# The first LayerNorm of an attention layer: where its statistics, power, scaling and maxima stand in the issue order

## What is computed

```
x = layernorm(x + local_attention(x))   # 16 heads of 64, q and k normed, rotary, windows of 128
x = layernorm(x + int8_linear(x))       # its input scale is max(abs(x)) over all of x
x = layernorm(x + linear_attention(x))
x = layernorm(x + bitlinear_ffn(x))
```

## Time and profile before

| | |
|---|---|
| median of three runs | 3080.65 us |
| profiled execution: its own time, its span | 3083.32 us, 3081.5 us |
| PE, DVE, ACT, POOL busy | 2928.3, 2364.4, 2176.6, 1663.0 us |
| PE busy as a share of the span | 95% |
| chain that ended last: PE, ACT, DVE | 21%, 8%, 4% of the span |
| TensorE clock granted | 0.988 of full speed over the span |

### The profile page before, as it was taken

One profiled execution on the slowest core, in us unless ns is written; L12 is line 12 of the kernel. 1 busy time (PEld: TensorE's weight loads), 2 busy tenths in 40 slices (PEclk: granted clock), 3 DMA queues, 4 the chain that ended last, 5 costly groups with the idle time before them and its releaser, 6 DMA issues. The chain is left out here.

```text
span 3081.5 us, 60397 instructions
## 1 busy us (share of the span) xinstructions
PE 2928.3 (95%) x20143; PEld 2313.1 (75%) x20143; DVE 2364.4 (77%) x6845; ACT 2176.6 (71%) x5670; POOL 1663.0 (54%) x2226
## 2 busy tenths in 40 slices
PE   7999999999999999999999996899999999999996
PEld 5777777777777777777777774578888888888885
DVE  7887877877877877877877874787777777777775
ACT  5676766766766766766766763577888888888884
POOL 5655655655655655655655654344555555555555
PEclk9999999999999999999999998899999999999999
DMA  2000000000000000000000002000000000000000
GB/s 84 8 15 22 9 15 20 10 15 15 15 15 15 15 15 15 15 15 15 15 15 15 8 25 86 21 15 8 15 15 15 21 22 15 15 14 15 8 15 21
DMA packets 51219, 57.51 MB, mean 19 GB/s; under 512 B 3008, under 2 KB 48592, under 8 KB 50912
## 3 DMA queue, kind: packets, MB, share of 16 engines
q1 hardware_dynamic: 47904, 50.67, 5.1%
q10 hardware_dynamic: 3008, 2.98, 0.3%
HBM read 36.86 MB, written 16.78 MB: 17 GB/s over the span
## 5 line engine op out<-in xcount | busy, mean ns | idle before, releaser
L642 POOL TENSOR_SCALAR a_ex<-a_ex,a_rc 128x384 f32<-128x384 f32 (+1 forms) x1024 | 538.5, 538 | 551.3 <-DVE a_rc L542 551.3
L434 ACT ACTIVATE a_ex<-a_sm,a_nm 128x384 f32<-128x384 f32 (+1 forms) x1024 | 573.0, 562 | 57.9 <-DVE a_nm L535 40.2
L535 DVE CUSTOM_DVE_ANT_0 a_sm<-sc,a_mask,a_rn 128x384 f32<-128x384 f32 (+1 forms) x1024 | 530.2, 544 | 8.9 <-PE sc L303 8.9
L626 POOL TENSOR_TENSOR a_qr<-a_ra,a_rb 128x256 f32<-128x256 f32 x512 | 370.4, 734 | 227.5 <-DVE a_rb L515 227.4
L440 ACT ACTIVATE a_pt<-tp 128x256 f32<-128x256 f32 (+1 forms) x512 | 221.5, 433 | 283.8 <-PE tp L322 283.7
L267 PE MATMUL pj<-a_whi,a_xhi 128*128 128x384 f32 x1024 | 391.1, 382 | 8.4 <-DVE a_wlo L187 5.1
L1718 POOL TENSOR_TENSOR b_alo<-b_ring,b_ahi 128x512 fp32r<-128x512 f32 x128 | 169.5, 1325 | 414.0 <-DVE b_ring L1547 388.2
L267 PE MATMUL pj<-a_whi,a_xlo 128*128 128x384 f32 x1024 | 346.6, 338 | 0.0
L267 PE MATMUL pj<-a_wlo,a_xhi 128*128 128x384 f32 x1024 | 345.7, 338 | 0.0
L303 PE MATMUL sc<-a_kT,a_qT 64*64 64x256 f32 (+1 forms) x4096 | 307.9, 416 | 1.6 <-DVE a_nm L535 0.9
L332 PE MATMUL qk<-a_pt,a_v 128*64 128x384 f32 (+1 forms) x2048 | 305.6, 441 | 0.6 <-DVE a_pt L547 0.6
(11 more groups left out here) (234 smaller groups left out, 8007.2 us busy)
## 6 DMA issues: line engine op xcount, KB each, us to landing
a_xres<-x SPq DMA_DIRECT2D x16, 512.0 KB, 3.8
y<-a_res SPq DMA_DIRECT2D x16, 512.0 KB, 2.9
b_y<-y SPq DMA_DIRECT2D x16, 512.0 KB, 3.9
a_xin<-x SPq DMA_DIRECT2D x15, 512.0 KB, 3.8
out<-b_y SPq DMA_DIRECT2D x15, 512.0 KB, 2.9
a_xin<-wqkv SPq DMA_DIRECT2D x8, 256.0 KB, 2.6
a_stage<-wqkv SPq DMA_DIRECT2D x3, 384.0 KB, 9.1
a_ot<-wqkv ACTq DMA_DIRECT2D x3, 384.0 KB, 12.0
```

The lines of the kernel that those rows point to most:

```text
L434: e.activation(ex[h][w][:, 0:width], sm[h][w % 2][:, 0:width], ACT.Exp, bias=nm[:, w, h:h + 1], scale=-1.0, accum_out=rs[:, w, h:h + 1]).t ...
L535: e.tensor_tensor_reduce(out=sm[h][w % 2][:, 0:width], in0=SC[w % 2][h][:, 0:width], in1=mem['mask'][:, off:off + width], scale=rn[:, par, ...
L626: e.tensor_tensor(qr[par][:, t, :].rearrange(half, h=4, s=2), ra[:, t % 2, :].rearrange(half, h=4, s=2), rb[:, t % 2, :].rearrange(half, h ...
L642: e.tensor_scalar(row, row, 0.0, rc[:, w, h:h + 1], ALU.add, ALU.mult).then_inc(g['exn_pool'], 1)
```

## The change

Within a batch after the first, the statistics of tiles 2 and 3 stay at the end of (1,0); the aggregation and the two small instructions behind it move to the end of (2,0). The power and shift on POOL move from the end of (1,1) into (2,1), behind that half body's first rotation. ACT's scaling moves from the end of (2,0), where it was four tiles in a row, to (3,1) and (4,1), two tiles each, one ahead of the first evacuation of weights and one behind it. The maxima move to the ends of (5,0), (6,0), (7,0) and (7,1). In every half body with u = 1 ACT's rounding of x (`act_x`) now stands behind its first evacuation of weights, not ahead of it; that has an effect in (5,1) and (6,1) of batches 0 to 14. In the last batch SP stores batch 14 behind the first four pieces of the weights.

```diff
--- before.py
+++ after.py
@@ -60,21 +60,25 @@
         small = {f'{name}_{k}': [P, TT] for k in ('ve', 'rs', 'minus', 'shift')}
         return {name + '_bn': [P, TT, 6], name + '_mv': [P, TT, 2], **small}
 
-    def stats(self, e, unit, rows, tiles=range(TT)):
-        g = self.sems
+    def stats(self, e, unit, rows, tiles=range(TT), close=True):
         for t in tiles:
             last = e.bn_stats(self.bn[:, t, :], rows[:, t, :])
         if tiles[-1] == TT - 1:
-            last.then_inc(g['st_dve'], 1)
-            e.wait_ge(g['st_dve'], 2 * unit + 1)
-            for t in range(TT):
-                last = e.bn_aggr(self.mv[:, t, :], self.bn[:, t, :])
-            last.then_inc(g['st_dve'], 1)
-            e.wait_ge(g['st_dve'], 2 * unit + 2)
-            if due(unit):
-                e.wait_ge(g['shift_pool'], unit)
-            e.tensor_scalar(self.minus[:, :], self.mv[:, :, 0], -1.0, None, ALU.mult)
-            e.tensor_scalar(self.ve[:, :], self.mv[:, :, 1], LN_EPS, None, ALU.add).then_inc(g['var_dve'], 1)
+            last.then_inc(self.sems['st_dve'], 1)
+            if close:
+                self.aggregate(e, unit)
+
+    def aggregate(self, e, unit):
+        g = self.sems
+        e.wait_ge(g['st_dve'], 2 * unit + 1)
+        for t in range(TT):
+            last = e.bn_aggr(self.mv[:, t, :], self.bn[:, t, :])
+        last.then_inc(g['st_dve'], 1)
+        e.wait_ge(g['st_dve'], 2 * unit + 2)
+        if due(unit):
+            e.wait_ge(g['shift_pool'], unit)
+        e.tensor_scalar(self.minus[:, :], self.mv[:, :, 0], -1.0, None, ALU.mult)
+        e.tensor_scalar(self.ve[:, :], self.mv[:, :, 1], LN_EPS, None, ALU.add).then_inc(g['var_dve'], 1)
 
     def rstd(self, e, unit):
         g = self.sems
@@ -474,17 +478,19 @@
             act_evacuate_weights(e, i + 1, w + 1)
             if ahead:
                 act_exp(e, next_i + 1, next_w + 1, 1)
-            if at.at(2, 0) and not at.first:
-                norm.apply(e, at.b - 1, mem['res'])
         else:
             if at.has_pair(2):
                 act_project(e, n + 2, (p + 2) % PAIRS, 1)
+            if p in (3, 4) and not at.first:
+                norm.apply(e, at.b - 1, mem['res'], (2 * p - 6,), False)
+            act_evacuate_weights(e, i, w)
+            if p in (3, 4) and not at.first:
+                norm.apply(e, at.b - 1, mem['res'], (2 * p - 5,), p == 4)
             if not at.last:
                 if at.at(5, 1):
                     act_x(e, at.b + 1, 0)
                 if at.at(6, 1):
                     act_x(e, at.b + 1, 1)
-            act_evacuate_weights(e, i, w)
             if ahead:
                 act_exp(e, next_i, next_w, 0)
             if at.has_pair(2):
@@ -554,9 +560,9 @@
                 e.wait_ge(g['y_out'], 16 * seq)
         e.tensor_tensor(halves(mem['res'], k), QK[:, :], halves(mem['xres'], k), ALU.add).then_inc(g['op_dve'], 1)
 
-    def dve_stats(e, seq, k):
+    def dve_stats(e, seq, k, close=True):
         e.wait_ge(g['op_dve'], 2 * seq + k + 1)
-        norm.stats(e, seq, mem['res'], (2 * k, 2 * k + 1))
+        norm.stats(e, seq, mem['res'], (2 * k, 2 * k + 1), close)
 
     def dve_amax(e, seq, t):
         if t == 0:
@@ -612,11 +618,13 @@
             if u == 1 and at.has_pair(2):
                 dve_rotate(e, n + 2, w)
         if at.at(1, 0) and not at.first:
-            dve_stats(e, at.b - 1, 1)
+            dve_stats(e, at.b - 1, 1, False)
+        if at.at(2, 0) and not at.first:
+            norm.aggregate(e, at.b - 1)
         if at.first and (at.at(0, 1) or at.at(2, 1)):
             dve_weights_low(e, 3 + p // 2)
         if not at.first:
-            for t, step in enumerate(((2, 1), (3, 0), (3, 1), (4, 0))):
+            for t, step in enumerate(((5, 0), (6, 0), (7, 0), (7, 1))):
                 if at.at(*step):
                     dve_amax(e, at.b - 1, t)
 
@@ -656,6 +664,8 @@
             pool_k_norm(e, n + 1, (p + 1) % 2)
         if u == 1 and at.has_pair(2):
             pool_rotate(e, n + 2, p % 2, 1)
+        if at.at(2, 1) and not at.first:
+            norm.rstd(e, at.b - 1)
         if at.has_next() and u == 1 and spare(i + 1):
             if at.has_pair(2):
                 pool_rotate(e, n + 2, p % 2, w)
@@ -666,8 +676,6 @@
                 pool_softmax(e, at.next_window + 1, at.next_w + 1)
             if at.has_pair(2):
                 pool_rotate(e, n + 2, p % 2, w)
-        if at.at(1, 1) and not at.first:
-            norm.rstd(e, at.b - 1)
         if at.first and (at.at(0, 1) or at.at(2, 1)):
             pool_weights_low(e, 3 + p // 2)
         if w1_piece(at) is not None:
@@ -709,10 +717,11 @@
                 keep(b + 1)
                 store(b)
             keep(B - 1)
-            store(B - 2)
             e.wait_ge(g['xt_pe'], 2 * B)
             raw = io['wqkv1'][:, DC:3 * DC, :].rearrange('p k n -> p (k n)')
             for k in range(W1_COUNT):
+                if k == 4:
+                    store(B - 2)
                 if k >= 2:
                     e.wait_ge(g['w1_pool'], k - 1)
                 e.dma_start(w1_raw[k % 2], raw[:, w1_columns(k)]).then_inc(w1_in[k % 2], 16)
```

## The result

The changed kernel takes 3057.31 us (median of six runs, 3054.51 to 3057.73) against 3080.53 (six runs): a ratio of 0.9921, 95% interval 0.991 to 0.9932, or 23 us less. The direction and the range of the prediction held, but it forecast 36.7 us, so 13.5 us are missing. The time lies 0.7 us under the upper end of the range, 3058. The profiled execution took 3057.54 us, with a span of 3055.7.

The account below looks back on a forecast made before the run. PE was taken as the bound, busy for 95% of the span. LayerNorm moves of -42.0 us and 5.3 us lost to the later x gave -36.7 us, from 3080.65 to 3043.9 us; range 3037 to 3058.

Parts of the forecast that it names:

- The LayerNorm's three moves: Aggregation leaves (1,1), power its end, scalings (2,0): saves 0.86, 0.85, 1.09 us in (1,1), (2,0), (2,1); 42.0 us in all.
- The arithmetic by covers: An engine's lateness costs PE only beyond a cover; for DVE's rotation in u = 1 half bodies the cover is 0.54 us.
- The added steps at 0: Aggregation in (2,0), power in (2,1), scalings in (3,1) and (4,1), later maxima and SP's store: each taken to cost 0.
- x in (5,1): x comes 0.70 us later, PE's spare transposes wait for DVE's remainder: PE loses 0.45 us (0.30 to 0.51).
- x in (6,1) and (7,0): (6,1) loses 0.64 us, taken out of (7,0)'s idle 0.69; together they gain 0.10 us.
- an end of -0.64 us a batch: Lower end of the range given for (6,1) and (7,0) together, -0.64 to +0.15 us around a gain of 0.10.
- Rival A: In (5,1) the spare transposes don't wait for DVE's remainder, so the 5.3 us aren't lost: 3038.7 us; 13%.
- Rival B: DVE's small instruction behind the sums ends 0.54 us later; (4,0), (5,0), (6,0), (0,0) pay 0.2 each: 3056 us; 14%.
- C: From (5,1) on PE follows late ACT and DVE one for one: 34 us slower, 3115 us; 4%.
- D: A second cause behind each of the three waits gives most of the time back, staying within 0.2%; 3%.

Follow-up runs that it names:

- (6,1) alone: Changed kernel with x rounded behind the evacuation of weights in (6,1) only, ahead of it in (5,1): 3050.85 us, ratio 0.9907.
- the late wait: Changed kernel, pair 0's first projection reading x's second half waiting for the remainder only ahead of its third matmul: 3053.64 us, ratio 0.9911.

## Why the prediction came out as it did

- The LayerNorm's three moves: right, term by term. Forecast 0.86, 0.85 and 1.09 us a batch; the three half bodies fell by 0.85, 0.85 and 1.08, and the experiments on scaling and aggregation show each by itself. The arithmetic by covers fits: the aggregation in (2,1) took 989.37 - 988.71 = 0.66 us and not 1.07, since its second instruction took 0.29 and not 0.67, and the rotation starts 0.91 us behind the start of (2,1), 0.22 later than in the ordinary (4,1), within the cover of 0.54:

```profile
988.71 0.36 DVE L75 BATCH_NORM_AGGREGATE a_ln_mv<-a_ln_bn 128x2 f32<-128x6 f32 x4
989.11 0.29 DVE L80 TENSOR_SCALAR a_ln_minus<-a_ln_mv 128x4 f32<-128x4 f32 x1
...
989.37 0.41 DVE L520 TENSOR_TENSOR a_ra<-pj,a_rot 128x256 f32<-128x256 f32 x1
```

- The added steps at 0: right. POOL's power took 1.01 us inside the idle time, with 0.70 us of it left ahead of the next rotation. The second scaling made the small instruction behind the sums start 0.65 us behind (5,0), the maximum of (3,1) had made it 0.67; it ended at 0.88, and PE paid nothing.

```profile
991.19 1.01 POOL L88 TENSOR_TENSOR a_ln_rs<-a_ln_ve,a_half 128x4 f32<-128x4 f32 x1
...
993.18 0.73 POOL L634 TENSOR_TENSOR a_qr<-a_ra,a_rb 128x256 f32<-128x256 f32 x1 [0.70 <-DVE a_rb L521]
...
1020.22 0.23 DVE L529 TENSOR_SCALAR a_ss<-a_ss 128x16 f32<-128x16 f32 x1
```

- x in (5,1): right, 0.50 us against a forecast of 0.45. The remainder starts 3.16 us behind the start where it was 2.46, and the spare transposes wait for it:

```profile
1028.12 0.69 DVE L511 TENSOR_TENSOR a_xlo<-qk,a_xhi 128x512 fp32r<-128x512 f32 x1 [0.92 <-ACT a_xhi L417]
1028.96 0.41 PE L326 MATMUL qk<-s_ident,a_ex 128*128 128x128 f32 x2 [0.30 <-DVE a_xlo L511]
```

- x in (6,1) and (7,0): wrong, and this is the missing 13.5 us or nearly so. The step that failed is "that wait doesn't hang on these transposes: it goes back over DVE's reciprocals and ACT's exponentials to the two transposes at 1054.08". Those transposes did come sooner, by 0.17 us, and q's transposes in (7,0) came 0.69 later all the same, counted from the start of (6,1). The chain goes through the projection behind them. In ACT's order v and the square of that projection stand ahead of the next exponentials, and the trace of before has ACT idle 1.27 us for it. The projection itself waits for the remainder (`xl_dve` in `pe_project`, for pair 0, tile 2):

```profile
1053.59 0.69 DVE L505 TENSOR_TENSOR a_xlo<-qk,a_xhi 128x512 fp32r<-128x512 f32 x1 [0.20 <-ACT a_xhi L413]
1054.33 0.44 PE L267 MATMUL pj<-a_whi,a_xhi 128*128 128x384 f32 x1
1055.69 0.28 ACT L418 ACTIVATE a_v<-pj 128x128 f32<-128x128 f32 x1 [1.27 <-PE pj L267]
```

With x 0.7 us later the projection starts 1041.97 - 1038.06 = 3.91 us behind the start of (6,1), where it was 1054.33 - 1051.13 = 3.20. ACT's square, the exponentials and in the end (7,0)'s wait shift by the same. I forecast a gain of 0.10 us a batch for the two half bodies, and they cost 0.69 - 0.01 = 0.68: 0.78 x 15 = 11.7 us. The experiments on (6,1) alone and on the late wait show it. Another 0.05 us a batch is (5,1) and 0.02 the LayerNorm's moves, about 1 us together; the last 0.7 us or so the runs don't settle.
- The loss in (6,1) was forecast as 0.64 and measured as 0.69, with a different wait named. The wait that the prediction named exists and is as late, as the late wait shows, so the size was near for a chain that wasn't the last to end.
- That the time falls into the range is owed to an end, not to the forecast. The prediction gave (6,1) and (7,0) together an end of -0.64 us a batch, which is (7,0) giving nothing back, and 0.68 was lost: 3043.9 + 0.74 x 15 = 3055. It named no rival and no chance for this, though, and the last 2 us under 3058 were room for late sums, which didn't occur.
- Rival A (x is free) is refuted by the kernel with x behind alone. Rival B (late sums) came nearest in time, 3056, for the wrong reason: it put the loss into (4,0), (5,0), (6,0) and (0,0), and they are clean. The kernel with both scalings behind shows that it wouldn't decide even with 0.45 us of lateness. C and D are refuted by the half bodies.
- The trace of before showed this wait, though without a bracket. DVE's remainder in (6,1) ends at 1053.59 + 0.69 = 1054.28, and the projection starts at 1054.33, 0.05 us later. In the changed kernel, where the profile names the remainder as what ended the wait, the lag is the same (1041.22 + 0.69 = 1041.91, then 1041.97). So the projection had no slack before the change either: every bit by which x came later had to reach it. A further sign is that the projection follows the two transposes of 1054.08 by 0.25 us, while the projection behind the last transposes, which waits for nothing, follows by 0.14 (1055.49, then 1055.63).

## What to carry to other kernels

Where a hand-ordered program repeats, cut its trace into the repeated bodies: a body's length over that of its clean neighbour is the price of what was put there, and these prices added up to within 0.1 us a batch. A short wait can stand in a trace without a bracket. So when a producer is moved later, list every wait on its semaphore in the code, and for each compare the end of the producer with the start of the consumer: a difference as small as where the profile does name the wait means that there is no slack. And idle time further on takes up a delay only if its own chain doesn't pass through what was delayed.

## What the runs showed of the hardware

In batch 8 a DVE instruction on four or sixteen elements took 0.17 us alone and up to 0.67 beside POOL. Where it was longer, it ended 0.02 to 0.03 us behind the end of the POOL instruction that had begun before it: in the changed kernel it was 0.29 us at 989.11, against the first of two scalings on POOL, from 988.90 to 989.37. Ahead of batch 0, beside a POOL instruction of 1.8 us, it took 1.47. Where two POOL instructions stood back to back it ended with the first of them, in every case read here, so that its price is the rest of one instruction and not of the queue. I had not expected how little depended on it: 0.45 us of lateness at that place cost PE 0.03.
